# The down product moved one step later in the expert pipeline, with the PSUM banks dealt out anew

## The reference

```python
x = x + attention(layernorm(x))          # x: 8 x 512 tokens of 128 numbers, as 16 x 256
xf = layernorm(x).reshape(4096, 128)
probs = softmax(xf @ router_w)           # 16 experts
w, idx = top_k(probs, 2)
keep = rank_of_token_in_expert < 640     # per choice, in the order of tokens
w = where(keep, w, 0)
# xe: the tokens of each expert
gate = xe @ gate_w[e]; up = xe @ up_w[e] # 128 x 128 each
out = (silu(gate) * up) @ down_w[e]
x = x + sum over both choices of w * out
```

## Time and profile before

| | |
|---|---|
| median of three runs | 263.82 us (263.49 to 264.31) |
| profiled execution, its own time | 263.7 us |
| span of its instructions | 261.1 us |
| mean granted TensorE clock | 0.789 of full |
| PE busy | 161.3 us (62%) |
| DVE busy | 151.9 us (58%) |
| POOL busy | 138.2 us (53%) |
| ACT busy | 97.1 us (37%) |

### The profile page before, as it was taken

One profiled execution on the slowest core, in us unless ns is written; L12 is line 12 of the kernel. 1 busy time (PEld: TensorE's weight loads), 2 busy tenths in 40 slices (PEclk: granted clock), 3 DMA queues, 4 the chain that ended last, 5 costly groups with the idle time before them and its releaser, 6 DMA issues.

```text
span 261.1 us, 4314 instructions
## 1 busy us (share of the span) xinstructions
PE 161.3 (62%) x979; PEld 137.5 (53%) x979; DVE 151.9 (58%) x746; ACT 97.1 (37%) x313; POOL 138.2 (53%) x154
## 2 busy tenths in 40 slices
PE   6397648559569549563588497648649586484000
PEld 5276536447457428452587486638548485373000
DVE  5459946936827817587084274737536447447463
ACT  2277436556455336345034133334234134133000
POOL 3001745736746735657556576656856675557400
PEclk9569968977956965975779869988977959869655
DMA  4997101111111122111324254234533646321863
GB/s 115 308 291 194 54 31 42 51 33 41 47 37 41 51 75 73 41 41 51 74 62 109 65 130 114 77 109 149 151 97 88 218 106 189 100 73 31 240 207 99
DMA packets 33144, 26.79 MB, mean 103 GB/s; under 512 B 4668, under 2 KB 29505, under 8 KB 33120
## 3 DMA queue, kind: packets, MB, share of 16 engines
q1 hardware_dynamic: 24944, 16.35, 23.8%
q0 software_dynamic: 4352, 8.47, 9.5%
q10 hardware_dynamic: 3824, 1.71, 2.3%
HBM read 14.57 MB, written 12.47 MB: 104 GB/s over the span
## 4 chain that ended last, share of the span: by engine, by line
PE 30%; issue 24%; ACT 11%; DVE 10%; another core or an unknown queue 10%; SPq 5%; PEld 4%; PEldq 2%; DMA 2%; DVEq 0%; POOL 0%; ACTq 0%; POOLq 0%
PE bank L1197 7%; PE bank L1099 4%; PE bank L1209 4%; PE bank L1078 3%; PEld bank L1197 2%; ACT xn L460 2%; PE bank L1091 2%; PE bank L1180 2%; PE bank L1084 2%; PE bank L1069 2%; PE bank L1042 2%; SPq L311 1%; DMA yg<-expert_results 1%; ACT vsb L453 1%
## 5 line engine op out<-in xcount | busy, mean ns | idle before, releaser
L424 POOL DMA_INDIRECT expert_results<-ye,dst x72 | 72.3, 1004 | 45.1 <-ACT ye L567 27.0
L410 POOL DMA_INDIRECT expert_rows<-xf,slots x64 | 63.3, 989 | 61.5 <-DVE slots L730 35.4
L874 DVE TENSOR_TENSOR hT<-sg,bank 128x256 f32<-128x256 f32 x36 | 15.1, 418 | 52.7 <-ACT sg L556 34.1
L1197 PE MATMUL bank<-xeT,ew 128*128 128x128 f32 x224 | 36.7, 316 | 8.6 <-issue 3.6
L1197 PEld LDWEIGHTS bank<-xeT,ew 128*128 128x128 f32 x224 | 33.3, 228 | 11.5 <-issue 6.9
L556 ACT ACTIVATE sg<-bank 128x256 f32<-128x256 f32 x36 | 13.9, 387 | 45.6 <-PE bank L1197 24.9
L1091 PE MATMUL bank<-vsb,ksb 128*128 128x145 f32 x64 | 15.1, 369 | 22.8 <-issue 13.9
L1209 PE MATMUL bank<-ew,hT 128*128 128x128 f32 x112 | 20.5, 311 | 13.6 <-DVE hT L874 8.6
L1091 PEld LDWEIGHTS bank<-vsb,ksb 128*128 128x128 f32 x64 | 11.3, 238 | 27.2 <-issue 16.0
L1209 PEld LDWEIGHTS bank<-ew,hT 128*128 128x128 f32 x112 | 17.1, 218 | 15.3 <-DVE hT L874 9.5
L567 ACT ACTIVATE ye<-bank 128x256 f32<-128x256 f32 x36 | 13.8, 386 | 22.8 <-PE bank L1209 14.4
(11 more groups left out here) (164 smaller groups left out, 311.1 us busy)
## 6 DMA issues: line engine op xcount, KB each, us to landing
xe<-expert_rows SPq DMA_DIRECT2D x72, 65.0 KB
yg<-expert_results SPq DMA_DIRECT2D x16, 256.0 KB, 3.4
xs<-in_L_attn_x_dram SPq DMA_DIRECT2D x2, 768.0 KB, 10.1
out_dram<-yg ACTq DMA_DIRECT2D x11, 128.0 KB, 1.9
expert_results<-ye,dst POOLq DMA_INDIRECT x72
expert_rows<-tailrows SPq DMA_DIRECT2D x17, 65.0 KB, 4.7
expert_rows<-xf,slots POOLq DMA_INDIRECT x64
out_dram<-yg SPq DMA_DIRECT2D x5, 128.0 KB
```

Of the source, the lines that this page charges most:

```text
L410: nc.gpsimd.indirect_dma_start(out=xbuf, out_offset=bass.IndirectOffsetOnAxis(ap=slots[:, col:col + 1], axis=0), in_=xf[:, t, :], in_offse ...
L424: nc.gpsimd.indirect_dma_start(out=y2, out_offset=bass.IndirectOffsetOnAxis(ap=dst[:, v:v + 1], axis=0), in_=ye[:, v, :], in_offset=None, ...
L874: nc.vector.tensor_tensor(hT[:, p % 2, :], sg[:, p % 2, :], banks[2 + p % 2][:, 2 * P:4 * P], ALU.mult).then_inc(B["hT"], 1)
L1197: ins = mm(banks[2 + p % 2][:, (2 * c + u) * P:(2 * c + u + 1) * P], weights_of(i, 2 * p + u)[:, c * D:(c + 1) * D], xeT[:, p % 2, u * P:( ...
```

## The change

The pipeline in `in_turns` gets a fourth place. PE's and ACT's third stage now takes pair m-3 instead of m-2, so a down product is issued after gate and up of the pair two later. `hT` gets four buffers. PSUM is dealt out anew: bank 0 alone holds transposes, banks 2 to 5 gate and up, banks 1 and 6 the down products, bank 7 both halves of the ranks, one after the other. With it the waits: a transpose waits for the copy of the pair before it instead of the one two before, gate and up wait for `hT` of four pairs earlier, `silu` waits for `hT` of two pairs earlier (since `sg` keeps two buffers), and the second half of the ranks is computed later. `under` becomes bfloat16.

```diff
-        under = sb("under", [P, HALF, K, E])
+        under = sb("under", [P, HALF, K, E], BF16)
...
-        hT = sb("hT", [P, 2, 2 * P])
+        hT = sb("hT", [P, PAIRS, 2 * P])
...
-            for m in range(PAIRS * STATIC + 2):
-                step([(divmod(m - k, PAIRS) if 0 <= m - k < PAIRS * STATIC else None) for k in range(3)])
+            for m in range(PAIRS * STATIC + 3):
+                step([(divmod(m - k, PAIRS) if 0 <= m - k < PAIRS * STATIC else None) for k in range(4)])
             with eng.Fori(STATIC, turns_of(eng)) as i:
-                for m in range(PAIRS + 2):
-                    step([((i, m - k) if 0 <= m - k < PAIRS else None) for k in range(3)])
+                for m in range(PAIRS + 3):
+                    step([((i, m - k) if 0 <= m - k < PAIRS else None) for k in range(4)])
...
             def xeT_copy(i, p):
...
-                nc.scalar.activation(xeT[:, p % 2, :], banks[p % 2][:, 0:2 * P], ACT.Copy).then_inc(B["xeT"], 1)
+                nc.scalar.activation(xeT[:, p % 2, :], banks[0][:, 0:2 * P], ACT.Copy).then_inc(B["xeT"], 1)
...
             def silu(i, p):
...
+                if not isinstance(i, int) or 4 * i + p >= 2:
+                    act.wait_ge(B["hT"], pairs_to(act, i, p - 1))
+                    held(act, i)
...
             def step(now):
-                for stage, pair in zip((xeT_copy, silu, y_copy), now):
+                for stage, pair in zip((xeT_copy, silu, y_copy), (now[0], now[1], now[3])):
...
-                if now[1] == (4, 0):
+                if now[1] == (4, 1):
                     under_capacity(1)
-                if now[1] == (4, 1):
+                if now[1] == (4, 2):
                     kept_tokens(1)
-                if now[1] == (4, 2):
+                if now[1] == (4, 3):
                     kept_weights()
...
-                pe.wait_ge(T["lasts"], 1)
-                r = banks[6 + h][:, 0:HALF * K * E]
+                pe.wait_ge(T["over"], 1)
+                need(pe, T["under"], h)
+                r = banks[7][:, 0:HALF * K * E]
...
             def transposed(i, p):
...
-                if not isinstance(i, int) or 4 * i + p >= 2:
-                    pe.wait_ge(B["xeT"], pairs_to(pe, i, p - 1))
+                if not isinstance(i, int) or 4 * i + p >= 1:
+                    pe.wait_ge(B["xeT"], pairs_to(pe, i, p))
...
             def gate_up(i, p):
...
-                if not isinstance(i, int) or 4 * i + p >= 2:
-                    pe.wait_ge(B["hT"], pairs_to(pe, i, p - 1))
+                if not isinstance(i, int) or i > 0:
+                    pe.wait_ge(B["hT"], pairs_to(pe, i, p + 1 - PAIRS))
...
-                        ins = mm(banks[2 + p % 2][:, (2 * c + u) * P:(2 * c + u + 1) * P],
+                        ins = mm(banks[2 + p][:, (2 * c + u) * P:(2 * c + u + 1) * P],
...
             def down(i, p):
...
+                if isinstance(i, int) and (i, p) == (0, 1):
+                    pe.wait_ge(T["left"], 1)
...
-                    ins = mm(banks[4 + p % 2][:, u * D:(u + 1) * D], hT[:, p % 2, u * P:(u + 1) * P],
+                    ins = mm(banks[1 + p % 2 * 5][:, u * D:(u + 1) * D], hT[:, p, u * P:(u + 1) * P],
...
             def step(now):
-                for stage, pair in zip((transposed, gate_up, down), now):
+                for stage, pair in zip((transposed, gate_up, down), (now[0], now[1], now[3])):
...
-                if now[0] == (3, 0):
+                if now[0] == (4, 1):
                     ranks_by_choice(1)
```

More of the change, by code:

```diff
@@ L555, in silu @@
                 held(act, i)
-                nc.scalar.activation(sg[:, p % 2, :], banks[2 + p % 2][:, 0:2 * P], ACT.Silu).then_inc(B["sg"], 1)
+                if not isinstance(i, int) or 4 * i + p >= 2:
+                    act.wait_ge(B["hT"], pairs_to(act, i, p - 1))
+                    held(act, i)
+                nc.scalar.activation(sg[:, p % 2, :], banks[2 + p][:, 0:2 * P], ACT.Silu).then_inc(B["sg"], 1)
             def y_copy(i, p):
@@ L566, in y_copy @@
                 held(act, i)
-                nc.scalar.activation(ye[:, v:v + 2, :], banks[4 + p % 2][:, 0:2 * D].rearrange("p (b d) -> p b d", b=2),
+                nc.scalar.activation(ye[:, v:v + 2, :], banks[1 + p % 2 * 5][:, 0:2 * D].rearrange("p (b d) -> p b d", b=2),
                                      ACT.Copy).then_inc(B["ye"], 1)
             def step(now):
-                for stage, pair in zip((xeT_copy, silu, y_copy), now):
+                for stage, pair in zip((xeT_copy, silu, y_copy), (now[0], now[1], now[3])):
                     if pair is not None:
@@ L873, in hidden @@
                 held(dve, i)
-                nc.vector.tensor_tensor(hT[:, p % 2, :], sg[:, p % 2, :], banks[2 + p % 2][:, 2 * P:4 * P], ALU.mult).then_inc(B["hT"], 1)
+                nc.vector.tensor_tensor(hT[:, p, :], sg[:, p % 2, :], banks[2 + p][:, 2 * P:4 * P], ALU.mult).then_inc(B["hT"], 1)
             def blocks_of_batches():
@@ L949, in under_capacity @@
                 dve.wait_ge(T["rank_ps"], h + 1)
-                ranks = banks[6 + h][:, 0:HALF * K * E].rearrange("p (t k e) -> p t k e", t=HALF, k=K)
+                ranks = banks[7][:, 0:HALF * K * E].rearrange("p (t k e) -> p t k e", t=HALF, k=K)
                 nc.vector.scalar_tensor_tensor(out=under[:, :, :, :], in0=ranks, scalar=float(CAP),
@@ L1179, in transposed @@
                     v = slot_of(i, 2 * p + u, XR)
-                    ins = nc.tensor.transpose(banks[p % 2][:, u * P:(u + 1) * P], xe[:, v, 0:D], ident[:, :])
+                    ins = nc.tensor.transpose(banks[0][:, u * P:(u + 1) * P], xe[:, v, 0:D], ident[:, :])
                 ins.then_inc(B["xeT_ps"], 1)
```

## The result

The changed kernel took 269.84 us (median of four runs, 268.02 to 271.29), the one before 264.06 us beside it (263.49 to 264.71): a ratio of 1.0192, 95% interval 1.013 to 1.0254. So it was slower there, by 5.8 us where +1.0 was forecast, and outside the range.

What follows compares the result with a forecast made beforehand. No engine was full; a ring of waits among PE, ACT and POOL was taken to bound it. Terms -1.65 + 1.65 + 1.0 = +1.0 us gave 264.7 profiled, 264.8 us forecast; range 261.4 to 267.2, 8 in 10.

Steps and rivals of the forecast that it cites:

- I take +1.0: End of the kernel: scatters some 1.3 us later, PE's own list 0.4 earlier; the scatters were taken to decide.
- That is 1.55 later: Loop's turn: down of pair 32 issued at 234.80 instead of 233.25, at down(33)'s place less one down product.
- the end follows the scatters: End: PE's count of landings ends when the scatters do, not with PE's own list; 1.3 later against 0.4 earlier.
- They belong to the work, and the change takes none away: Second part: stretches of some 3 us with PE's results unseen by others were taken as given, unchanged in number.
- the silent stretches: Second part: some 3 us each in which other engines do not see PE's results; one down product would fall into each.
- 0.0 (-4.1 to +2.2): Written-out turns: 1.65 us gained on gate and up cancels 1.65 lost by transposes waiting on the single bank.
- under 3 us: Second part: PE's waits for `hT` before down products fall from 12.0 us to under 3.
- Waits before gate and up for `ew`: Second part: these waits on PE would appear in place of those for `hT` before down; no size given.
- less than 1: Written-out turns: gate and up of pair 22 start less than 1 us ahead of 195.17, 0.95 to gain.
- rival 1: Turns: weights don't decide, DVE gets ahead, each silent stretch takes in a down product; 260.9 us, or 262.5; chance 27%.
- a little of the clock: Whole kernel: small clock share added to rival 1's 27%, making 0.29 for faster by over 0.3%.
- Gives it back: Start: transposes move ahead of the first down, PE waits for DVE's table of rows and recovers it; no cost.

Runs made afterwards that it cites:

- C3: Profile of the changed kernel, run word for word a third time, on chip 5: 275.86 us, 1.0126 times the kernel before.
- C2: Profile of the changed kernel, run again word for word on chip 10: 274.15 us, 1.0123 times the kernel before.
- the lag alone: Kernel before with down of pair m-3, four `hT` buffers, `under` in bfloat16, old banks: 1.0001 on chip 6, 1.0179 on chip 10.
- B2: Profile of the kernel before, unchanged, run against itself on chip 10: 270.15 us, ratio 1.0138.
- the one pause: Changed kernel, POOL waiting once, before pair 30's scatters, for its last scatter's landing: 0.999, 1.0237, 0.9902 times the kernel before; also put in the kernel before: 1.0113.
- the pauses in all turns: POOL waits after every four scatters for its last one's landing: in the changed kernel 1.0135, in the kernel before 1.0244, both against the kernel before.

## Why the prediction was wrong

**The place was right: the end of the written-out turns.** The step that failed is the term "I take +1.0" of the end, resting on "That is 1.55 later", and it failed by its size. I priced one step of delay as PE's work: down of pair 32 at the place of down of pair 33. But the steps between the two places wait for copies, and these are held back when POOL scatters: the copy of pair 32 in the first profile and C3, that of pair 34 in C2 and with the lag alone. From gate and up of pair 31, down of pair 32 came 5.8 us later on the mean of three profiles each (18.0 and 12.3), where I had 1.55. From pair 27's scatters to pair 32's the change cost 3.1 us (21.46 - 18.33), and 4.9 in the first two. A longer run of scatters is not the reason. The changed list has three down products in a row at its tail, and the run was of ten scatters in its first profile and in C3, but of ten in B2 as well and of eight in C2. What the change moved is what has to wait behind it. The end gives some back (25.5 us from pair 32's scatter to the end before, 24.3 after, means of three): net from pair 27 on it is 45.75 - 43.86 = +1.9 us, where I had +1.0. That the end follows the scatters was right: in the chain that ended last PE's counting runs until about 255.9 us in the changed kernel, and the last scatter began at 253.68.

**"They belong to the work, and the change takes none away" was the wrong way to look at the silent stretches.** They hang on POOL's runs, at least in good part. In the changed kernel's timeline POOL's run ends with a scatter at 172.13, it is idle, and ACT and SP come to life at once, 1.14 us after that scatter's end:

```profile
172.13 0.98 POOL L424 DMA_INDIRECT expert_results<-ye,dst  x1 [0.30 <-issue]
...
174.25 0.38 ACT L559 ACTIVATE sg<-bank 128x256 f32<-128x256 f32 x1 [3.92 <-remote]
```

In the earlier trace rows it was alike: the stretch ended at 164.46, and POOL's run with a scatter that began at 162.74 and took 0.98. POOL stops for want of `ye`, and `ye` waits for the stretch to end. I read the two as one loop, which in the changed kernel repeated about every 9.5 us, three pairs at a time (164.76 and 174.25 are two such ends). What sets its length was not tested by itself.

**The written-out turns: right within their bounds.** I had 0.0 (-4.1 to +2.2). From pair 0's to pair 27's scatter the first two profiles gave +1.5, the means of three +1.6. The waits for `hT` went (I had said under 3 us; the page gives 0.6 us before down in all, for `ye`) and those before transposes came (13.7 + 7.5 = 21.2 us; I had said 5 or more). Waits before gate and up for `ew` did not appear: 6.1 us stand there with nothing named. Gate and up of pair 22 ran 59.4 us after the first scatter, 62.3 before, which looks like 2.9 us gained, and I had said less than 1. But the other profiles gave 58.9 and 60.3 with the change, 61.5 and 58.1 without, so no run shows that PE or DVE got ahead, and rival 1's mechanism is not shown. Between the first transposes and pair 32's scatter PE's idle time was 38.1, 37.6 and 41.1 us with the change, 34.9, 36.8 and 34.7 without, so it rose by 3.5 on the means, not within 1.5. (Taken from 121 to 240 us, as I had said, it rose by 4.8, but 4.7 us of the changed kernel's part one fall into that window.)

**The clock.** The chances took in "a little of the clock" for the faster side; no run shows such a gain. In the changeover the clock went against the change: granted 0.69, 0.76 and 0.68 with it, 0.80, 0.80 and 0.73 without.

**"Gives it back" at the start: not always.** This term was put at nothing. The transposes that move ahead of the first down product are those of pair 3, not the third as I wrote, and gate and up of pair 2 move with them. Where a stretch begins there, they all wait, as in C2:

```profile
129.40 1.29 PE L1201 MATMUL bank<-xeT,ew_sb 128*128 128x128 f32 x8
134.08 0.66 PE L1184 MATMUL bank<-ident,xe 128*128 128x128 f32 x2 [3.39 <-ACT xeT L551]
134.53 1.91 PE L1201 MATMUL bank<-xeT,ew_sb 128*128 128x128 f32 x8
136.24 1.06 PE L1215 MATMUL bank<-ew_sb,hT 128*128 128x128 f32 x4
```

The first down product came 8.4 and 8.8 us after the first transposes in two profiles with the changed lists, 10.0 in two and 11.8 to 12.2 in four; in seven with the lists before, 7.4 to 10.2. It costs nothing or some 3 us. The kernels with the one pause have the same instructions as the others up to pair 30, so they can be counted in: from the first transposes to the first scatter the mean is 12.5 us in six profiles of the changed kernel and 10.3 in four of the kernel before, and from there to pair 27's scatter 88.6 and 86.7. So the start and the turns cost some 2 us each, as far as such spreads allow (single profiles at the start: 9.7 to 14.0 us with the change, 8.8 to 11.8 without).

**How much of the miss that explains.** The means of three make part two 5.1 us longer, against a measured +5.8, and put it on the start (+1.7), the turns (+1.6) and the end (+1.9), where I had 0.0, 0.0 and +1.0. The first two profiles put it otherwise: 4.7 of 7.0 us in part one, which the change doesn't touch. My sum was made as if everything outside the change repeated within 0.3%, since the three runs shown did. It doesn't: part one took 121.0 to 131.2 us on such chips. Whether the changed kernel's part one is always longer on the chip of the result was not tested, so how the 5.8 us divide there stays open.

## What to carry to other kernels

Price a step of delay by what stands between the old and the new place in the list, waits included, and look first at where a pipeline fills and runs empty: there the slack of the steady part is missing. Before a wait is taken as given, ask whose activity it lines up with; here it was the scatters of another engine, and one wait in the right place took back the changeover's loss. One trace of each kernel is not enough to say where the time went: a second and a third moved 4.7 us from one part to the other. And when a few runs agree to 0.3%, run the unchanged kernel against itself once; here it differed by up to 1.4%.

## What the runs showed of the hardware that was not expected

- While POOL issued indirect DMAs back to back (one in 1.28 us), results of PE were often not seen by ACT, DVE and SP until up to 1.7 us after the run's end (1.14 us above, 0.23 in C2; 6.6 us from the transposes at 229.26 to their copy at 235.90). It isn't strict: some got through within a run (ACT's `ye` at 233.03 in the changed kernel, 4.4 us late), and runs of four scatters held results too. Breaking the run brings them earlier (the one pause, and in part the pauses in all turns). What in the chip holds them was not found; on chip 6 POOL scattered for over 90 us with hardly a gap, and nothing was held.
- The kernel before took 217.6 us (median) on chip 6, 269.7 to 271.9 on chips 5, 10 and 15 and 264.1 beside the result, with nearly the same busy time of DVE, ACT and POOL (151.8, 99.4 and 141.2 us for the changed kernel on chip 6, 152.4, 97.2 and 137.6 in its first profile). POOL's DMAs show it from the first part on: the first came at 25.4 us in both, the 24th at 55.25 in the changed kernel on chip 6 and at 62.71 in the profile before. Why the chips differ stays open, and so does why the kernel before had so short a part one beside the result.
